# Maxima pass in four 64x64 tiles, eight bursts a head, and numerators by token halves

## The reference

```python
# layer 0: attention with relative positions
content_score = einsum('bthd,bshd->bhts', q + u_bias, k)
pos_score = _rel_shift(einsum('bthd,phd->bhtp', q + v_bias, p))
attn = softmax((content_score + pos_score) / sqrt(dh), axis=-1)
ctx = einsum('bhts,bshd->bthd', attn, v).reshape(b, t, d)
...
# layer 1: linear attention (q and k behind elu + 1)
kv = einsum('bnhd,bnhe->bhde', k, v)
z = 1.0 / (einsum('bnhd,bhd->bnh', q, k.sum(axis=1)) + 1e-06)
out = einsum('bnhd,bhde,bnh->bnhe', q, kv, z).reshape(B, N, D) @ wo + bo
```

## Time and profile before

| | us |
|---|---|
| median of 3 runs | 1076.53 |
| lowest, highest | 1075.40, 1077.13 |
| the profiled execution | 1076.74 |
| its span on the core | 1074.9 |

### The profile page before, as it was taken

One profiled execution on the slowest core, in us unless ns is written; L12 is line 12 of the kernel. 1 busy time (PEld: TensorE's weight loads), 2 busy tenths in 40 slices (PEclk: granted clock), 3 DMA queues, 4 the chain that ended last, 5 costly groups with the idle time before them and its releaser, 6 DMA issues.

```text
span 1074.9 us, 21825 instructions
## 1 busy us (share of the span) xinstructions
PE 853.6 (79%) x8587; PEld 648.4 (60%) x8587; DVE 722.4 (67%) x1573; ACT 460.1 (43%) x773; POOL 397.3 (37%) x446
## 2 busy tenths in 40 slices
PE   2483679999999999987558998999999687147774
PEld 1243468888888888875435655565666376025553
DVE  6672435565555655533577898978788587989994
ACT  3860023333333333334455555666556544322331
POOL 6463001333334334325433334434343206323544
PEclk7696689999999999988669999999999799579997
DMA  5057211333333323363100000000000000000111
GB/s 139 1 157 216 42 38 42 76 76 65 66 92 74 71 65 74 87 154 70 25 1 1 2 1 2 1 2 2 1 1 1 1 1 1 0 0 4 21 26 30
DMA packets 69743, 46.45 MB, mean 43 GB/s; under 512 B 35184, under 2 KB 60984, under 8 KB 68920
## 3 DMA queue, kind: packets, MB, share of 16 engines
q1 hardware_dynamic: 52776, 24.72, 10.0%
q0 software_dynamic: 8032, 19.11, 7.0%
q10 hardware_dynamic: 8832, 1.22, 0.7%
HBM read 30.05 MB, written 12.06 MB: 39 GB/s over the span
## 4 chain that ended last, share of the span: by engine, by line
PE 43%; DVE 26%; DMA 8%; SPq 6%; ACT 6%; issue 5%; POOL 5%; ACTq 0%; POOLq 0%; DVEq 0%
PE PS L1058 7%; PE PS L1173 5%; PE PS L1175 5%; PE PS L1174 5%; PE PS L1078 4%; PE PS L1038 4%; PE PS L1062 4%; PE PS L1039 3%; SPq L349 2%; DMA REG<-inverse_sums 2%; DVE HB L1786 2%; DVE REG L1581 2%; DVE XX L1446 2%; DVE XX L1452 2%; DVE AM L1437 2%
## 5 line engine op out<-in xcount | busy, mean ns | idle before, releaser
L1562 DVE TENSOR_REDUCE MX<-PS 128x2 f32<-128x512 f32 x256 | 171.2, 685 | 172.6 <-PE PS L1039 171.3
L776 ACT ACTIVATE REG<-PS 128x1024 f32<-128x1024 f32 x128 | 131.6, 1028 | 241.4 <-PE PS L1062 238.6
L1058 PE MATMUL PS<-XX,TB 96*128 96x64 f16 x2048 | 160.3, 246 | 7.8 <-DMA XX<-NEG 4.5
L1038 PE MATMUL PS<-TM,YY 128*128 128x256 f16 x512 | 129.1, 284 | 33.7 <-DMA YY<-REG 16.6
L1058 PEld LDWEIGHTS PS<-XX,TB 96*128 96x128 f16 x2048 | 133.8, 120 | 23.5 <-issue 12.8
L613 POOL TENSOR_TENSOR HH<-HB,HH 128x512 f16<-128x512 f32 x64 | 75.6, 1182 | 172.3 <-ACT HH L833 172.3
L1039 PE MATMUL PS<-KM,YY 128*128 128x256 f16 x512 | 126.2, 278 | 0.0
L863 ACT ACTIVATE SG<-PS 128x512 f32<-128x512 f32 x128 | 76.2, 595 | 110.3 <-PE PS L1175 110.0
L1786 DVE SCALAR_TENSOR_TENSOR HB<-PS,SG 128x512 f32<-128x512 f32 x128 | 87.3, 682 | 44.4 <-ACT SG L863 44.4
L1062 PE MATMUL PS<-XX,KC 97*128 97x128 f16 x1024 | 107.8, 229 | 0.0
L1173 PE MATMUL PS<-XH,XX 128*128 128x512 f16 x256 | 98.1, 383 | 10.0 <-DVE HB L1786 9.7
(11 more groups left out here) (235 smaller groups left out, 1659.5 us busy)
## 6 DMA issues: line engine op xcount, KB each, us to landing
REG<-inverse_sums POOLq DMA_DIRECT2D x60, 128.0 KB, 2.9
YY<-queries_content ACTq DMA_DIRECT2D x224, 4.0 KB
KC<-keys_strips SPq DMA_DIRECT2D x16, 192.0 KB
keys_strips<-REG POOLq DMA_DIRECT2D x12, 224.0 KB, 7.8
R<-in_L_attn_x SPq DMA_DIRECT2D x32, 64.0 KB, 2.7
queries_position<-REG POOLq DMA_DIRECT2D x2, 960.0 KB, 13.9
queries_content<-REG POOLq DMA_DIRECT2D x2, 960.0 KB, 18.3
XX<-queries_position SPq DMA_DIRECT2D x60, 32.0 KB
```

The lines of the kernel that those rows point to most:

```text
L776: A(P[jt][:, 1024 * up:1024 * up + 1024].rearrange("p (k x) -> p k x", k=2), ST[u % 2], ACT.Exp).then_inc(exp_done, 1)
L1038: mm(o, yp[:, a], TM[p][:, 31 - a:31 - a + T], start=True, stop=False)
L1058: mm(o_pos[:, a], TB[p][0:96, y0:y0 + 128], xp[0:96, 8 * bank + a], start=(a == 0), stop=False, skip_group_check=True)
L1562: nc.vector.tensor_reduce(MX[h % 2][:, 2 * kk:2 * kk + 2], banks[4 + kk % 2].rearrange("p (a j) -> p a j", a=2), AX_X, ALU.max)\
```

## The change

- **Maxima pass.** `YP` and `YC` are half as long (`N // 2` columns). Rows 0 to 63 hold batches 0 to 7, rows 64 to 127 batches 8 to 15 (`r`). A 64-row stationary of 64 columns now covers 8 batches x 8 blocks, and the two column halves of the array (`c`) take two different offsets a, 16 apart. One burst g makes four offsets: twice (i) four position matmuls and four content matmuls, one in each 64x64 tile, each with 256 moving columns. It fills two banks (`maximum_banks`: 4 and 5; for head 0 by turns also 6 and 7). Eight bursts a head, 128 matmuls instead of 64.
- **VectorE** takes one reduction 128x1024 to 128x4 a burst: 8 a head instead of 16. A burst waits for the reduction of the burst just before it (`max_done`, n), since there is one pair of banks.
- **Order.** Bursts stand behind the even k (0 to 14); the second-half context of head h-1 behind k = 3. `BANKS` is reordered so that k = 0 to 3 need only the first half of the shift row; the second is waited for at k = 4. Evacuation stands behind reduction 2, the inverse behind reduction 6.
- **Loads.** `TM` gets two DMAs. SP loads `YP` rows 0 to 63 in eight DMAs of 64 pieces; rows 64 to 127 come by ACT for head 0 and by POOL for the others (`later_queries`, eight DMAs between L553's and L559's in each head). A shift row half is four DMAs of 64 pieces instead of one of 128, the second half at u = 7 instead of u = 6. `XC` is laid out so that its loads are contiguous.
- **Weights.** SP's expert loads wait for the last maxima, now behind k = 14 of head 14 (before: k = 11).
- **Second attention.** A numerators chunk is four batches of one token half. Output products 0 to 2 stand between the numerators from chunk 5 on, gates 0 and 1 behind quotients 6 and 7. The gates write to `EX` instead of `CT`.

```diff
-BANKS = (0, 4, 1, 5, 2, 6, 3, 7)
+BANKS = (0, 4, 2, 6, 1, 5, 3, 7)
...
+        def maximum_queries(eng, h, src, half, done):
+
+            for s in range(8):
+                rows = 64 * half + 8 * (7 - s)
+                eng.dma_start(YP[h % 2][rows:rows + 8, :].rearrange("p (n s a) -> p s n a", n=8, s=8)[:, s],
+                              src[:, N // 2 * half:N // 2 * half + N // 2].rearrange("p (n s a) -> p s n a", n=8, s=8)[:, s])\
+                    .then_inc(done[h % 2], 16)
+
+        def maximum_banks(h, g):
+
+            return 6 if h == 0 and g % 2 else 4
...
+                row = XC[n % 2][96:97, :].rearrange("p (r m c t a) -> p r c t m a", r=2, m=64, c=2, t=2)
+                for r in range(2):
+                    for c in range(2):
+                        act.dma_start(row[:, r, c, half], NEG[half][64 * c:64 * c + 64, 8 * r:8 * r + 8]).then_inc(neg_in[half], 16)
...
+                if g == 0:
+                    pe.wait_ge(y_in[p], Y_FIRST[p] + Y_LOADS * (h // 2))
+                    if h:
+                        pe.wait_ge(y_second[p], Y_SECOND * ((h + 1) // 2))
+                if h:
+                    pe.wait_ge(max_done, n)
+                elif g >= 2:
+                    pe.wait_ge(max_done, g - 1)
...
+                for i in range(2):
+                    tiles = [(slice(64 * r, 64 * r + 64), 16 * c + 2 * g + i, banks[bank + r][64 * c:64 * c + 64, T * i:T * i + T])
+                             for r in range(2) for c in range(2)]
+                    for rows, a, o in tiles:
+                        mm(o, yp[rows, a], TM[p][rows, 31 - a:31 - a + T], start=True, stop=False)
+                    for rows, a, o in tiles:
+                        last = mm(o, yc[rows, a], KM[p][rows, :], start=False, stop=True)
                 last.then_inc(max_mm, 1)
...
-                    if h + 1 < H and k < 12:
-                        for kk in range(16 * k // 12, 16 * (k + 1) // 12):
-                            maximum_scores(h + 1, kk)
-                    if h and k == 4:
+                    if h + 1 < H and k % 2 == 0:
+                        maximum_scores(h + 1, k // 2)
+                    if h and k == 3:
...
+                nc.vector.tensor_reduce(MX[h % 2][:, :].rearrange("p (r a) -> p r a", r=2)[:, :, 2 * g:2 * g + 2],
+                                        PS[:, bank:bank + 2, :].rearrange("p r (i j) -> p r i j", i=2), AX_X, ALU.max)\
                     .then_inc(max_done, 1)
...
+            for c in range(8):
+                numerators(c)
+                if c:
+                    turn_attention(c - 1)
+                if c >= 5:
+                    output_products(c - 5)
+            turn_attention(7)
+            for c in range(3, 8):
+                output_products(c)
```

180 lines of the change are left out of this document (91 added, 89 removed).

## The result

| | before | after |
|---|---|---|
| median, us | 1076.48 (4 runs) | 1100.62 (4 runs) |
| lowest, highest | 1075.40, 1077.13 | 1097.86, 1106.37 |
| the profiled execution, its span | 1076.74, 1074.9 | 1100.53, 1098.7 |

The ratio is 1.0225, with a 95% interval of 1.0201 to 1.0249: the change makes the kernel 2.2% slower, where 1050 was forecast. The gain of 26 us became a loss of 24.

The account below looks back on a forecast made before the run. PE was taken to set the pace at 22.3 us a head, falling to 20.7 with GpSimd close behind; -22.4 - 1.6 - 4 + 1 + 3.5 - 2.7 = -26.2 gave 1050 us, forecast 1038 to 1062, range 1037 to 1072.

Parts of the forecast that it names:

- A burst: Maxima matmuls on PE: four groups of four at 0.11 plus 0.23 for the tile shape, 0.67 us; -1.7 a head.
- the first rival: Maxima bursts: weight loads or row halves don't overlap, groups take 0.22, head 23.9 us, time 1098; chance 0.12.
- The reduction: VectorE's 128x1024 reduction behind each burst: between 1.2 and 1.37 us, taken as 1.22.
- PE's head: PE's time for a steady head: 22.3 falls to 20.5 us (to 21.1).
- Head 15: Second shift half lands late among the expert loads: a stall of 5 to 8 us, +3.5 (0 to +7).
- Second attention: Gates among the quotients close a gap, output products hold up numerators: -4.4 + 1.7 = -2.7 us (0 to -4).
- 3.0 + 4.6 + 13.2 = 20.8 a head: GpSimd's chain with eight query DMAs added (4.6): 20.8 us a head, 0.3 behind PE's 20.5.
- Rival 2: GpSimd (head 22.0, time 1070) or the second shift half (1 us a head, 1064) becomes the bound; chance 0.26.
- The shift half needs some 5.8 us from the last burst, and k = 4 comes after 7.3.: Second half of the shift row arrives before k = 4; with 1.5 us more on ACT's queue each head waits, giving 1064.
- The start: Before head 0's maxima beside the scores: shorter SP query loads against eight more ACT DMAs, -4 us (-8 to +2).
- head 0: Head 0, with one context, gains 1.6 us from the shorter head.
- Head 1: Shares the gain 22.3 to 20.7; its first burst waits for head 2's content rows, four shift DMAs among them: +1 us.

Follow-up runs that it names:

- e8: Changed kernel with the shift row's second half not dependent on the last burst (row content wrong) and the queries' second half issued by SyncE; 1054.0 us.
- e14: e12 with two of the four DMAs of the shift row's second half issued by SyncE, nothing left out; 1063.8 us, ratio 0.9870.
- e4: Kernel before with only the second-attention part of the change; 1073.37 us, ratio 0.9962.
- e13: Kernel before with its eight query DMAs a head, from head 2 on, issued by GpSimd behind its sums instead of by SyncE; 1098.9 us.
- e3: Changed kernel with the second half of the maxima's position queries issued by SyncE instead of GpSimd; 1085.5 us.
- e1: Changed kernel with the shift row's second half carrying the first half's maxima, issued at u = 5, not dependent on the last burst (content wrong); 1089.9 us.
- e2: Changed kernel with only one of the four DMAs of each shift row half (row content wrong); 1084.9 us.
- e7: Changed kernel with bursts at k = 0, 2, 3, 4, 7, 9, 10, 12, row at u = 6, GpSimd's queries ahead of its wait for the sums' DMA; 1088.7 us.
- e9: Changed kernel with queries' second half on SyncE, last burst between the context halves, shift row's second half ahead of u = 6; 1118.7 us, ratio 1.0392.
- e12: e9 with the shift row's second half issued behind exponential u = 6 instead of ahead of it; 1073.4 us, ratio 0.9965.

## Why the prediction was wrong

**Right.** *A burst*: 0.67 foreseen, 0.66 found, groups 0.11 apart; the first rival (groups of 0.22, 1098) has nearly the time that came by luck, since its mechanism is absent. *The reduction*: 1.22 foreseen, 1.224 found. *PE's head*: 20.5 (to 21.1) foreseen; 20.8 where nothing else is late (e8), 21.2 in e14. *Head 15*: a stall of 5 to 8 us foreseen, 6.6 found, the head 2.2 longer where 3.5 was put. *Second attention*: -2.7 foreseen, -3.0 in the trace, -4.1 alone (e4).

**Wrong, GpSimd.** The step is "3.0 + 4.6 + 13.2 = 20.8 a head", with the inverse as the only one who might come to wait for it. The eight DMAs were sized right (4.45). The step asked how long the chain is, and not who waits for its parts and by when. The queries had been issued by SyncE well ahead of their reader (the last of them 6.6 us); in the change they stand behind an evacuation that comes in the middle of the head and a round trip, and the next head's first burst needs them. This alone costs 22 us in the kernel before (e13), and moving it back gives 15 (e3). Besides, the chain is longer than its sum: between 175 and 480 the wait for the sums' DMA is 3.05 us a round (39.7 in 13) where it was 1.95 (27.3 in 14), that for the broadcasts 4.9 (58.3 in 12) where it was 3.7 (47.9 in 13); a round has 0 to 1.6 us of idle time left where it had 1.6 to 5.7. With the row out of the way the chain's length is a bound itself: in e1 GpSimd has no idle time in nine of thirteen rounds, and heads are 23.4. Rival 2 had the engine, at 22.0 and with a chance of 0.26 for both its halves, but by the price of a DMA, which did not change.

**Wrong, the shift row.** "The shift half needs some 5.8 us from the last burst, and k = 4 comes after 7.3." The 7.3 is nearly right: in the head shown, the last burst begins at 282.86 and PE wants the row at 290.5, 7.6 us later. The need was mis-sized: from that burst to the landing it is 9.6 us (0.8 to the reduction, 1.5 to the first issue, 1.8 to the start of the last, 5.5 to its landing), and nearly all of the difference is the landing, which had been taken at the median of the earlier trace rows, 2.1. The median of the changed kernel, 2.5, hides it, since it mixes two kinds: in heads 2 to 14 the DMAs of the row's first half land in 1.6 to 2.5 us, those of the second half, the same in size and number, in 3.2 to 5.9, and not only the last of the four (5.0, 5.0, 4.9 and 5.6 in head 2). The rival said "with 1.5 us more each head waits" and priced 1 us a head; twelve of thirteen heads did wait, for 1.8 on average, and the clock came on top.

**Wrong, the sum of the two.** Both cases were in the text with small prices, since each was priced as the time that PE stands. Behind seven of the fifteen waits for row or queries in heads 2 to 14 the clock fell to 1.2 GHz (waits of 1.8 to 4.3 us; behind others, of up to 2.1 us, it did not), and blocks then take 1.25 us in place of 0.68 until it is back; the heads with the longest such stretches are 28.8 and 27.2. Against the 20.7 foreseen a head, heads 2 to 14 took 44 us more: 27.3 are the waits, some 16 the clock, which the sum had at nothing. In the same heads of e8 and e14, where no wait is longer than 1.7 and 0.9 us, the clock is full throughout.

**Wrong, the start.** -4 foreseen, and -1.6 for head 0. Its k = 0 starts 5.7 us later (129.3 against 123.6), and it is 5.5 us shorter, since the wait of 4.9 us that stood behind its k = 0, for SyncE's queries of head 1 (until 129.9), is gone: +0.1 for both. Head 1, for which the terms gave 0.6 less, takes 1.35 more; its first burst waits for the content rows, which land at 160.8, at 160.0 before. Half the pieces per DMA did not help: SyncE's eight took 18.2 us in place of 20.2, with all DMA engines busy at that time, and ScalarE's eight queries stand behind sixteen content rows that took 29.7 us to issue:

```profile
76.12 29.71 ACTq L778 DMA_DIRECT2D YY<-REG  x16
105.85 5.97 ACTq L300 DMA_DIRECT2D YY<-NQB  x8
```

The first maxima of head 0 began at 113.4 in place of 107.8. I had added ScalarE's eight DMAs as 0.7 each and forgotten what they queue behind.

**What stays open.** Why the row's second half takes up to 5.9 us to land. It isn't only the number: a single DMA takes 3.1 to 5.7 there (e2), and the first half's four take 1.6 to 2.5. That the four broadcasts (128 KB each) meet it was my explanation, and e3 can't tell, since both moved together. The landing times over all runs speak for it. Where the first broadcast is issued 0.4 to 1.7 us ahead of the row, all four DMAs of the row take 3.5 us or more (the changed kernel and e3). Where the row goes some 1 us ahead, its first DMA lands in 1.6 to 1.7 us in nearly all heads of e7, e9 and e12, and the last in 4 to 7. Where the two lie 5 us or more apart, the last DMA of the second half takes 1.8 to 3.8 (e1, e8). But in four heads of the changed kernel the row goes 0.6 to 1.0 us ahead and its first DMA still takes 3.4 to 4.2, and no run moves the broadcasts alone: this is a correlation, not a cause shown. GpSimd's pauses between two issues (2.8 us in the changed kernel, 1.6 and 2.2 in e13) are open too.

## What to carry to other kernels

When a load moves to another engine's queue, ask two things of its new place: what must have happened before it can be issued, and when the first reader wants it; the engine's sum of work answers neither. A wait for several DMAs goes by the last one's landing, and a median over the whole run mixes quiet places with busy ones, so price it by the rows of DMAs that are issued beside the same traffic. When two edits each give little, try them together before giving up the cause: here 11 and 15 us singly were 47 together. And a stop of PE can cost more than its length, by the clock behind it: here 27 us of waits brought some 16 more.

## What the runs showed of the hardware

- 64x64 tiles in both row groups run four at once as closely as a single 128x128 matmul: groups 0.11 us apart, weight loads hidden, though two tiles share a row group. The Trainium skill, TensorE: Matmul & The Clock Gate, Part 3, has loads overlap only across row groups; the rows of the result speak against it for two column tiles in one.
- GpSimd's issue of a DMA hardly depends on its pieces: eight of 64 take 4.45 us, eight of 128 4.72 (e13). ScalarE's row DMAs went from 0.48 us for one of 128 pieces to 0.60 each for four of a quarter of the data.
- With the DMA engines all busy (DMA share 1.01 from 75 to 95 us) a DMA on SyncE takes 2.3 us to issue with 64 pieces and 2.5 with 128; in the heads, at a share of 0.3 to 0.4, the form with 64 takes GpSimd 0.56.
- A small DMA can take more than twice as long to land beside large ones, at a mean DMA share of 0.4: in the changed kernel the row's 1 KB DMAs took 1.6 to 2.5 us in the quiet part of the head, 3.4 to 5.9 in the twelve heads where the broadcasts were issued within 1.6 us of them, and 3.2 to 3.4 in the one where they followed 5.2 us later.
